# Second attention layer on one NeuronCore: V blocks of 512 queries behind the first score pair, turnings behind the second

## The reference

```python
q = _split_heads(_lin(hidden_states, Wq, bq))
k = _split_heads(_lin(hidden_states, Wk, bk))
v = _split_heads(_lin(hidden_states, Wv, bv))
scores = jnp.einsum('bhsd,bhtd->bhst', q, k) * SCALE
attn = jax.nn.softmax(scores, axis=-1)
ctx = jnp.einsum('bhst,bhtd->bhsd', attn, v)
output = _lin(_merge_heads(ctx), Wo, bo)
rq = _split_heads(_lin(output, Wrq, brq))
rk = _split_heads(_lin(past_states, Wrk, brk))
rv = _split_heads(_lin(past_states, Wrv, brv))
rscores = jnp.einsum('bhsd,pbhtd->pbhst', rq, rk) * SCALE
rattn = jax.nn.softmax(rscores, axis=-1)
rctx = jnp.einsum('pbhst,pbhtd->pbhsd', rattn, rv)
recursive_output = _merge_heads(rctx).mean(axis=0)
gate = jax.nn.sigmoid(_lin(jnp.concatenate([output, recursive_output], axis=-1), Wg, bg))
output = output * (1.0 - gate) + recursive_output * gate
```

## Time and profile before

| | us |
|---|---|
| median of 3 runs | 940.89 |
| lowest, highest | 940.39, 941.63 |
| span of the profiled execution | 918.6 |
| attention of the second layer in it | from 350.1 to about 765 |

### The profile page before, as it was taken

One profiled execution on the slowest core, in us unless ns is written; L12 is line 12 of the kernel. 1 busy time (PEld: TensorE's weight loads), 2 busy tenths in 40 slices (PEclk: granted clock), 3 DMA queues, 4 the chain that ended last, 5 costly groups with the idle time before them and its releaser, 6 DMA issues.

```text
span 918.6 us, 19243 instructions
## 1 busy us (share of the span) xinstructions
PE 852.7 (93%) x6883; PEld 543.4 (59%) x6883; DVE 733.2 (80%) x2133; ACT 585.7 (64%) x1277; POOL 279.3 (30%) x423
## 2 busy tenths in 40 slices
PE   7799999998788899999999999999999999888994
PEld 6456666565488875445444544445454444888993
DVE  6888888888457787997989887988999984787774
ACT  2457676666556526798879877878777876343331
POOL 7123232425511445402310020201105622335332
PEclk9899999999979998999999998999999996979997
DMA  4424320011112113800000000000071100102123
GB/s 138 108 60 139 98 65 24 13 25 30 43 30 84 53 38 115 277 2 2 2 1 2 2 1 2 1 1 1 1 256 44 49 1 16 45 26 81 49 71 108
DMA packets 47927, 48.38 MB, mean 53 GB/s; under 512 B 5606, under 2 KB 39398, under 8 KB 47576
## 3 DMA queue, kind: packets, MB, share of 16 engines
q1 hardware_dynamic: 39784, 38.03, 14.2%
q0 software_dynamic: 3296, 6.82, 2.3%
q10 hardware_dynamic: 4752, 2.30, 0.8%
HBM read 30.83 MB, written 21.02 MB: 56 GB/s over the span
## 4 chain that ended last, share of the span: by engine, by line
PE 65%; DVE 24%; issue 3%; POOL 3%; ACT 2%; DMA 2%; SPq 0%; DVEq 0%; POOLq 0%; ACTq 0%
PE pv L1781 15%; PE st L1758 9%; PE ring L1749 9%; DVE M L2082 7%; PE ring L1650 5%; PE ring L1895 5%; PE st L1650 4%; PE st L1880 3%; DVE M L2089 3%; DVE ring L2086 3%; PE ring L1661 2%; PE ring L1711 2%; PE st L1873 2%; PE st L1888 2%; PE pv L1888 1%
## 5 line engine op out<-in xcount | busy, mean ns | idle before, releaser
L1507 ACT ACTIVATE Et<-st 128x512 f32<-128x512 f32 (+3 forms) x768 | 374.0, 551 | 121.0 <-PE st L1758 117.0
L2089 DVE TENSOR_REDUCE M<-ring 128x1 f32<-128x512 f32 x256 | 160.1, 683 | 29.3 <-PE ring L1749 29.2
L2082 DVE TENSOR_REDUCE M<-ring 128x2 f32<-128x512 f32 x256 | 159.9, 681 | 13.4 <-PE ring L1749 13.0
L2086 DVE CUSTOM_DVE_ANT_0 ring<-ring,maskw 128x128 f32<-128x128 f32 (+3 forms) x256 | 121.8, 509 | 24.4 <-PE ring L1749 23.0
L1781 PE MATMUL pv<-Et,Va 128*32 128x256 f32 (+3 forms) x1536 | 136.4, 416 | 1.8 <-POOL Et L1321 1.6
L1749 PE MATMUL ring<-Kbd,Qa 128*128 128x128 f32 (+3 forms) x256 | 88.6, 368 | 9.7 <-DVE M L2086 6.7
L1321 POOL TENSOR_SCALAR_AFFINE_SELECT Et<-Et 128x256 f32<-128x256 f32 x128 | 53.2, 418 | 135.2 <-ACT Et L1507 133.4
L1758 PE MATMUL st<-Qb,Kbd 128*128 128x512 f32 (+3 forms) x256 | 84.6, 351 | 4.9 <-ACT Et L1507 4.6
L1781 PE MATMUL pv<-Et,RV 128*32 128x256 f32 x1024 | 86.4, 409 | 1.0 <-ACT PVs L1514 1.0
L1749 PE MATMUL ring<-RKT,Qa 32*128 32x512 f32 x256 | 80.7, 504 | 4.3 <-DVE M L2082 2.6
L1758 PE MATMUL st<-Qb,KT 32*128 32x512 f32 x256 | 75.6, 506 | 0.0
(11 more groups left out here) (295 smaller groups left out, 1515.4 us busy)
## 6 DMA issues: line engine op xcount, KB each, us to landing
Xd<-Xd SPq DMA_DIRECT2D x8, 1056.0 KB, 16.7
L1W<-in_L1W SPq DMA_DIRECT2D x2, 2048.0 KB, 12.4
Kbd<-Ksb SPq DMA_DIRECT2D x60, 64.0 KB, 2.0
Xs<-Xd SPq DMA_DIRECT2D x39, 66.0 KB, 1.9
W<-in_L0W SPq DMA_DIRECT2D x8, 258.0 KB, 3.9
W<-in_L0W SPq DMA_DIRECT2D x8, 256.0 KB, 4.2
G<-Zd SPq DMA_DIRECT2D x8, 256.0 KB, 4.1
Yd<-Yt ACTq DMA_DIRECT2D x30, 64.0 KB, 1.6
```

Source lines behind the costliest of these rows:

```text
L1507: e.activation(Et[s // 2 % 4][:, j % 2, q0:512], bank(ph)[:, q0:512], ACT.Exp, scale=SCALE).then_inc(exp_done, 1)
L2082: e.tensor_reduce(M[i][:, t, j, :], bank(ph)[:, :].rearrange("p (two n) -> p two n", two=2), AX.X, ALU.max).then_inc(mx_red, 1)
L2086: e.tensor_tensor_reduce(bank(ph)[:, 0:n], bank(ph)[:, 0:n], maskw[:, 512 - n:512], 1.0, -3e38, ALU.add, ALU.max, M[i][:, t, j, 0:1]).then ...
L2089: e.tensor_reduce(M[i][:, t, j, 0:1], bank(ph)[:, 0:n], AX.X, ALU.max).then_inc(mx_red, 1)
```

## The change

In the second layer the two half V blocks become one: `pva` is gone, and `pv` runs over all 512 queries, behind the first score pair of the next key tile. Behind the second pair stands no V work. The waits between the steps of the turnings, projections and past states are set so that they fall behind second pairs: `KPREP` for the second layer goes from 5 to 3, `FINISH` from 5 to 3, `prep_qkv` and `past_prep` take two steps where they took one, and the start steps of some phases move by one or two. The first layer's values stay as they are. `PREP` was not used.

```diff
-KPREP, QPREP, FRONT, BACK = (2, 5), 7, (10, 12), (34, 36)
-AFTER_MAX, FINISH, PREP = (4, 3), (2, 5), (-24, -23)
+KPREP, QPREP, FRONT, BACK = (2, 3), 7, (10, 12), (34, 36)
+AFTER_MAX, FINISH = (4, 3), (2, 3)
...
-STEPS1 = {("self", 1): 41, ("rec", 0): 111, ("self", 2): 169, ("rec", 1): 239, ("self", 3): 297, ("rec", 2): 367, ("rec", 3): 431,
+STEPS1 = {("self", 1): 39, ("rec", 0): 111, ("self", 2): 167, ("rec", 1): 239, ("self", 3): 295, ("rec", 2): 367, ("rec", 3): 431,
...
@@ prep_qkv
-        yield
+        yield from wait(l + 1)
         for t in range(4):
             do("qkv", l, b, k, t)
-            yield
+            yield from wait(l + 1 if t < 3 else 1)
         do("qkv2", l, b, k)
@@ back
             do("st", l, u, c, 1)
             yield
             if c:
-                do("pva", l, u, c - 1)
+                do("pv", l, u, c - 1)
             yield
             do("st", l, u, c, 2)
             do("st", l, u, c, 3)
-            yield
-            if c:
-                do("pv", l, u, c - 1)
-            yield
+            yield from wait(2)
         yield from wait((3, 1)[l])
-        if l:
-            do("pva", l, u, 3)
-            yield from wait(2 if u < 31 else 0)
         do("pv", l, u, 3)
@@ PE, the V block
-                    cols = slice(128 * c, 512) if l == 0 else slice(0, 256) if what == "pva" else slice(256, 512)
+                    cols = slice(128 * c if l == 0 else 0, 512)
...
-                        if j % 2 and what == "pv":
+                        if j % 2:
                             ins.then_inc(pv_half, 1)
```

More of the change, by code:

```diff
@@ L67 @@
           ("ln", 3): 136, ("route", 0): 186, ("route", 1): 234, ("route", 2): 296, "first": 240, "experts": 295, "next": 296}
-STEPS1 = {("self", 1): 41, ("rec", 0): 111, ("self", 2): 169, ("rec", 1): 239, ("self", 3): 297, ("rec", 2): 367, ("rec", 3): 431,
-          ("blend", 0): 263, ("blend", 1): 391, ("blend", 2): 503, ("rows", 0): 331, ("route", 0): 406, ("route", 1): 522,
-          ("route", 2): 556, "weights": 424, "past": 59, ("ln", 1): 22, ("ln", 2): 148, ("ln", 3): 276, ("mod", 0): 100,
-          ("mod", 1): 124, ("mod", 2): 148, ("mod", 3): 172, "wipe": 60, "keys": 92, "first": 480, "experts": 550}
+STEPS1 = {("self", 1): 39, ("rec", 0): 111, ("self", 2): 167, ("rec", 1): 239, ("self", 3): 295, ("rec", 2): 367, ("rec", 3): 431,
+          ("blend", 0): 263, ("blend", 1): 391, ("blend", 2): 503, ("rows", 0): 331, ("route", 0): 407, ("route", 1): 522,
+          ("route", 2): 556, "weights": 424, "past": 57, ("ln", 1): 22, ("ln", 2): 148, ("ln", 3): 276, ("mod", 0): 100,
+          ("mod", 1): 124, ("mod", 2): 148, ("mod", 3): 172, "wipe": 60, "keys": 91, "first": 480, "experts": 550}
 def wait(n):
@@ L512, in past_keys @@
             do("pastK", g)
-            yield from wait((6, 14, 4, 4)[g])
+            yield from wait((8, 12, 4, 4)[g])
     def modulation(b):
@@ L1759, in _ @@
                                      start=True, stop=True).then_inc(st_full, 1)
-                elif what in ("pva", "pv"):
+                elif what == "pv":
                     l, u, c = a
@@ L1781, in _ @@
                         ins = nc.tensor.matmul(pv[32 * j:32 * j + 32, cols], v, Et[s // 2 % 4][:, j % 2, cols],
-                                               start=first and (l == 0 or what == "pva"), stop=done, skip_group_check=True)
-                        if j % 2 and what == "pv":
+                                               start=first, stop=done, skip_group_check=True)
+                        if j % 2:
                             ins.then_inc(pv_half, 1)
```

## The result

The changed kernel takes 950.26 us (median of 947.95, 948.75, 952.77 and 951.77), the kernel before on the same chip 941.26 (four runs, 940.39 to 942.03): 1.0125 of before, interval 1.0089 to 1.0161. It is slower, by 9.0 us of medians. The forecast was 938.6, the range 926 to 950; so the sign was wrong, and the time lies just outside.

What follows compares the result with a forecast made beforehand. PE and VectorE were taken to bound the kernel by turns, ScalarE close behind. Terms of -17.9 + 19.8 - 3.8 - 0.4 = -2.3 us took 940.9 to 938.6 us, range 926 to 950.

Steps and rivals of the forecast that it cites:

- The rest: Second layer's attention: moved key, row and norm turnings and GpSimd's (POOL's) work after a projection cost nothing.
- Spreading the projections: Projections behind every second pair feed VectorE more evenly, in three batches and at the stretch's start: -3.8 us.
- What bounds the kernel: Second layer's attention, 410.4 us: PE and VectorE take turns in ending last, ScalarE close behind.
- Whole V blocks: PE, second layer: one 1.00 us block replaces two halves of 1.14, saving 0.14 in each of 128: -17.9 us.
- The place of the block: Gaps behind second pairs: PE waits for score banks rise from 28 to 48 us, +19.8 us; unit 10 11.90 us.
- my sum: Attention, units 0 to 30: PE work saved, bank waits added, spreading and copy, together -2.3 us.
- The copy of the finished sum: ScalarE's copy follows the block at once: half of 5.6 us waits won, exponentials delayed +2.4 us; together -0.4.
- The clock: PE in the attention: one more stretch at the lower granted clock costs 2 to 5 us, one less returns them.
- The full gain: Rival: new bank waits lie beside existing waits; 919.2 us, or 929 if half are paid; full or half gain 0.20.
- Slower: Rival, chance 0.27: held scores also hold maxima, VectorE runs dry, turning gaps 1.72 us, no spreading gain; 950.7 us.
- The evacuation floor: Rival, chance 0.10: the engines emptying PSUM set the time; PE's waits only move, time stays at 940.9 us.
- What would show it: Signs: 1.00 us blocks, tiles 3.1, 2.6, 3.1, exponential waits 35 or more, units 8 and 9 shorter, 10 and 11 longer.

Runs made afterwards that it cites:

- early_proj: The changed kernel with the projections of batches 1 to 3 two to four score pairs earlier; 1.0016, 1.0070 and 1.0034 of the kernel before, on three chips.
- proj_old: The changed kernel with the second layer's projections one pair apart again, from steps 41, 169 and 297; 1.0057 of the kernel before.
- before_early: The kernel before with only the projections of batches 1 to 3 two pairs apart and six to eight steps earlier; 1.0036 of the kernel before.
- early_half: early_proj with half V blocks behind every pair; 1.0064 of the kernel before, and 1.0112 on another chip (early_half_b).
- before_narrow: The kernel before with half of the second layer's exponentials left out from unit 1 on; 0.9904 of the kernel before.
- early_free: early_proj with half of the second layer's exponentials and half of the maxima's columns left out; 0.9491 of the kernel before.
- block_only: Whole V blocks of the changed kernel with every spacing and start of the kernel before; 1.0117 of the kernel before.

## Why the prediction was wrong, point by point

**"The rest ... what POOL has to do after a projection moves with it. These I cost at nothing": this step failed.** It is the largest part of the miss that the runs can price. The evidence for nothing was that GpSimd is busy 90 of 410 us. The question was not its share but its distance: a chain of 3.9 us, after it a turning that had 7 pairs before and 3 after the change, so that PE waited 2.3 us twice and ran the unit behind at a lower clock. Taking the lateness away gives back 5.6 us (2 to 8) of a loss of 9 to 10. From the forecast of -2.3 to the measured +9.3 (mean of three comparisons) are 11.6 us, so this is about half of the miss. What is left, early_proj at +3.7 in place of -2.3, is unit 31 (2.6, below) and some 3 us that no run places.

**Spreading the projections, -3.8 us.** As made, it cost instead of gaining: proj_old, which takes it back, is 1.0057 against 1.0101 for after, some 4 us better (on different chips), and has no wait for GpSimd. That is the same failed step seen from the other side, since the spreading is what brings the last projection close to the turning. The gain itself depends on the block: with whole blocks and an early start about 2.6 to 3.9 us (early_proj against proj_old, not settled), with half blocks none (before_early, 3 us slower than before). Units 8 and 9 shrink from 27.4 us to 24.4 in early_proj and 25.8 in early_half, but early_half loses more than that in units 7, 14, 25, 26 and 30, and is 6 to 10 us slower than before.

**What bounds the kernel:** read rightly as PE and VectorE by turns, but not followed to its end. In plain units VectorE was within 0.2 to 0.4 us of being the only bound, as before_narrow (11.0 us) shows, and the sum added PE's savings and waits over all units as if PE's way alone counted. It came out level at 380 and 379 us, and the 31 us between that and the stretch of 410 were taken as fixed.

**Whole V blocks, -17.9 us.** The price of 0.14 us a block holds (0.99 to 1.00 us; 2.46 us for a tile in early_free). PE's busy time in the stretch fell by 5 to 12 us in early_proj.

**The place of the block, +19.8 us.** In the plain unit right to 0.2 us (12.11 for 11.90; before 11.3). The waits for exponentials went from 16 us to 27 or 28 (28 or 29 in early_proj): the right way, but short of the 35 forecast. What was over-counted are the units with more work (13, 16, 17, 21, 25, 26 are shorter with the whole block): there other work fills the waits. Net of the block my sum said +1.9; at the new spacing the runs say -4 to -6, at the old one +11. So there is no one price of the block.

**The copy of the finished sum, -0.4:** its waits are gone; no run priced it.

**Not in the sum at all:** from unit 31's first score on, 2.6 us on the mean for early_proj (0 to 4 by single profiles), whose cause stays open.

**The clock**, taken as a side remark of 2 to 5 us for a stretch: the mean granted clock in the attention went from 0.98 to 0.94 and 0.95. At 0.98 early_proj's stretch is 406.9 us, at 0.95 and 0.96 it is 410.9 and 410.4: about 4 us, so the size was fair. In units 10 and 18 it follows the waits for GpSimd and adds to their price; elsewhere what brings it is not shown (unit 8 of early_half_b took 17.1 us at 0.80 with PE busy throughout, 14.4 at 1.00 in early_half). It is not the cause of the whole: block_only lost 8 us at 0.99.

**The rivals.** The full gain is out. "Slower" gave 950.7, near the time, for other reasons: its terms (turning gaps of 1.72, VectorE dry 0.15 us a unit) would have made every plain unit long, and these are as forecast. The evacuation floor was right for the plain units in that nothing was won there, but the banks that it leaves out made them 0.8 us longer. The range ended at 950, and that the time came so near it is luck: the term that failed was in no rival.

**What would show it:** right were the block of 1.00, tiles with a turning in a score bank of 3.2, 2.9 and 3.1 us (the one with a sum's turning took 2.9 in place of 2.6), the score loads' waits up (but to 27 or 28 us and not 35), the copy's waits gone, unit 11 longer by 0.8. Wrong were the waits for maxima (33 to 68 us: two groups of maxima now stand close together, and VectorE takes 1.29 us for two banks), unit 10 longer by 2.0, and units 8 and 9 longer by 1.3 in place of shorter.

## What to carry to other kernels

When a producer is moved or spread out, walk its results through every engine to the first use, and compare the distance in queue steps before and after; an engine that is busy for a fifth of the time can still hold all the others. Before adding up what an edit saves on one engine, make the other engines lighter, in thought or in a run, and see whether the unit shortens: here 0.56 us less PE work in a unit of 11.3 us met a VectorE that is busy for 10.8 of them, and, with VectorE made light, a wait for the score banks. And an order that has been spaced for one shape of a step loses when the step changes alone: block and spacing each cost some 11 us by themselves, and after one more move of the projections both together were 0.2 to 0.7% above before. No version here that does all the work beats the kernel before.

## What the hardware showed beyond that

Chips differ by 2.0 to 2.5% for the same kernel (918.7 to 920.9 us on four, 939.0 and 941.3 us in the two comparisons on slower ones), and the profiles of other kernels say where. In all four profiles from the slower kind of chip a tile of unit 26 or 27 takes 7 to 15 us; in none of the fifteen from the faster kind, nor in that of before, does one take more than 5.7. At that place GpSimd issues a row of indirect DMAs, and PE, ScalarE and VectorE stop for something that the profile does not show. First profile of after:

```profile
725.74 0.95 POOL L1360 DMA_INDIRECT Xd<-fh,pos  x1 [0.30 <-issue]
...
731.43 0.60 ACT L1508 ACTIVATE PVs<-pv 128x512 f32<-128x512 f32 x1 [6.47 <-remote]
731.46 0.69 DVE L2076 TENSOR_REDUCE M<-ring 128x2 f32<-128x512 f32 x1 [6.86 <-remote]
```

The same kernel with half blocks on either kind of chip (early_half and early_half_b) differs by 17.9 us of span: 10.2 in units 24 to 27, and 8.5 behind unit 31's first score. Why is open, and no profile shows the kernel before on the slower kind.
